# Predicting the scale of a fp16 product one batch early in a pipelined cross-attention and feed-forward kernel

## What is computed

```python
qh = Wq @ layernorm(x)                 # 512 x 1024, 8 heads of 64
kh, vh = Wk @ ctx, Wv @ ctx
q = softmax(qh, axis=head dim) * 64**-0.5
k = softmax(kh, axis=tokens)
context = einsum('hdn,hen->hde', k, vh)
out = Wo @ einsum('hde,hdn->hen', context, q) + bo
x = x + out / max(norm(out, channels), 1e-12) * g * sqrt(128)
x = x + layernorm(x) @ dequant(qweight, scales, zeros) + bias
```

## Time and profile before

| | |
|---|---|
| median of 3 runs | 782.26 us (781.7 to 784.06) |
| the profiled execution, its own time | 783.55 us |
| its span in the trace | 781.7 us |
| busy PE / DVE / POOL / ACT | 84% / 76% / 65% / 55% |
| mean granted TensorE clock | 0.972 of full speed |

### The profile page before, as it was taken

The page is one execution under the profiler, slowest core; times in us unless marked ns, Lnnn a source line. Parts: engine busy times, 40 slices in busy tenths (PEclk is TensorE's granted clock), DMA queues, the critical chain, the costliest instruction groups (busy, mean ns, idle before and its releaser), DMA issues.

```text
span 781.7 us, 10910 instructions
## 1 busy us (share of the span) xinstructions
PE 654.3 (84%) x3271; PEld 418.1 (53%) x3271; DVE 597.3 (76%) x929; ACT 431.6 (55%) x676; POOL 510.3 (65%) x362
## 2 busy tenths in 40 slices
PE   2888888898898989889898889889898988989664
PEld 2655556565555656555555555555565655556231
DVE  2897768887887879787887988788788878877622
ACT  2786457475545656564565747455574755456320
POOL 3273757668585757859485785948577685866641
PEclk9989899999999999999999999999999999999796
DMA  8035263443528254352725345262625434252602
GB/s 296 27 63 127 54 155 49 113 104 68 162 54 188 44 128 97 64 150 54 188 54 159 56 82 141 51 183 54 174 42 108 119 61 114 54 135 42 141 7 81
DMA packets 180982, 78.94 MB, mean 101 GB/s; under 512 B 170440, under 2 KB 172000, under 8 KB 180960
## 3 DMA queue, kind: packets, MB, share of 16 engines
q1 hardware_dynamic: 180960, 78.68, 42.8%
HBM read 28.32 MB, written 8.39 MB: 47 GB/s over the span
## 4 chain that ended last, share of the span: by engine, by line
DVE 32%; PE 32%; issue 18%; POOL 10%; ACT 5%; DMA 1%; DVEq 1%; ACTq 0%; POOLq 0%; SPq 0%
PE ps_m L918 13%; DVE q_sum L691 6%; DVE q_nmax L679 6%; DVE k_nmax L672 5%; POOL q_exp L392 4%; DVE x2n_lo L731 3%; POOL rn L444 3%; DVE stats L753 2%; PE ps_o L1018 2%; DVE q_exp L684 2%; DVE g_lo L745 2%; PE ps_k L860 2%; ACT q_tok_hi L532 2%; PE ps_k L862 2%; PE ps_k L861 2%
## 5 line engine op out<-in xcount | busy, mean ns | idle before, releaser
L402 POOL TENSOR_TENSOR q_tok_lo<-q_exp,q_tok_hi 128x1024 f16<-128x1024 f32 x64 | 136.7, 2135 | 84.4 <-ACT q_tok_hi L532 84.4
L392 POOL TENSOR_TENSOR q_exp<-q_exp,q_rec 128x1024 f32<-128x1024 f32 x64 | 122.7, 1917 | 68.4 <-DVE q_rec L696 68.4
L521 ACT ACTIVATE q_exp<-q_exp 128x512 f32<-128x512 f32 x128 | 80.8, 631 | 150.5 <-DVE q_exp L684 150.2
L516 ACT ACTIVATE k_exp<-ps_k,k_nmax 128x1024 f32<-128x1024 f32 x64 | 71.2, 1113 | 122.4 <-DVE k_nmax L672 120.1
L918 PE MATMUL ps_m<-k_t,c_t 128*128 128x512 f32 x256 | 116.4, 598 | 0.0
L672 DVE TENSOR_REDUCE k_nmax<-ps_k 128x1 f32<-128x1024 f32 x64 | 77.9, 1217 | 39.2 <-PE ps_k L862 39.2
L971 PE MATMUL ps_m<-w_int,x_lo 128*128 128x512 f16 x240 | 93.9, 391 | 13.3 <-DMA x_lo<-x2n_lo 13.2
L679 DVE TENSOR_REDUCE q_nmax<-ps_q 128x8 f32<-128x512 f32 x128 | 86.6, 677 | 13.2 <-PE ps_q L862 13.1
L972 PE MATMUL ps_m<-w_int,x_hi 128*128 128x512 f16 x240 | 93.7, 391 | 0.0
L684 DVE TENSOR_TENSOR q_exp<-ps_q,q_nmax 128x512 f32<-128x512 f32 x128 | 88.5, 691 | 4.4
L425 POOL TENSOR_TENSOR c_lo<-c_in,c_hi 128x1024 fp32r<-128x1024 f32 x16 | 37.9, 2369 | 65.8 <-ACT c_hi L600 65.8
(11 more groups left out here) (126 smaller groups left out, 1437.5 us busy)
## 6 DMA issues: line engine op xcount, KB each, us to landing
x_in<-in_x SPq DMA_DIRECT2D x16, 512.0 KB, 5.7
c_in<-in_ctx SPq DMA_DIRECT2D x16, 512.0 KB, 6.4
x_res<-in_x SPq DMA_DIRECT2D x16, 512.0 KB, 4.9
out_x<-y SPq DMA_DIRECT2D x15, 512.0 KB, 3.4
q_hi<-q_tok_hi SPq DMA_TRANSPOSE x64, 3.1
q_lo<-q_tok_lo SPq DMA_TRANSPOSE x64, 3.0
og<-in_L_ffn_qweight SPq DMA_DIRECT2D x1, 512.0 KB, 5.3
sq<-in_L_ffn_qweight SPq DMA_DIRECT2D x1, 512.0 KB, 6.2
```

The source lines that it names most:

```text
L392: nc.gpsimd.tensor_tensor(pair, pair, rec.unsqueeze(2).to_broadcast([P, 2 * HEADS, DH]), ALU.mult).then_inc(qs_done, 1)
L402: nc.gpsimd.tensor_tensor(q_tok_lo[p % 2][:], q_exp[:, 2 * p:2 * p + 2, :].rearrange("p t d -> p (t d)"), q_tok_hi[p % 2][:], ALU.subtract ...
```

## The change

G's scale is no longer taken from G. k's softmax weights sum to one, so no entry of M is larger, once normalised, than the largest absolute context value (`c_top`), and G sums 128 channels against `vo`: 128 x `c_top` x `v_top` (the largest absolute value in `vo`) bounds it. `v_top` is found once in turn 0 (two DVE reductions, one PE transpose). `c_top` is found for batch n in turn i: DVE reduces `c_in` to `c_abs` (1024 elements), PE spreads it (`spread_c`), DVE reduces the row. `fit_g` works out the scale of batch a in five small DVE operations, and `k_rec` carries it. In the next turn `g_hi` is written by DVE straight from PSUM (ACT's L595 goes), and `g_lo` by four DVE operations of 128 elements from PSUM. `g_t`, the reduction L741 and `spread_g` go. `c_hi` and `c_lo` have one buffer instead of two.

Each engine's order within a turn is new (K0' is the first k projection of batch n, M[a:b] are M's token tiles, c3 is the query pair 3 of batch c, a0 to a2 are pairs 0 to 2 of batch a):

| engine | before | after |
|---|---|---|
| PE | K0 Q0 TC0 G, K1 Q1 TC1 spread_g F0, K2 TK0 Q2 TK1 O0, K3 TK2 Q3 TK3 O1, TK4 Q4 TK5 F1a norm, TK6 Q5 TK7 F1b rn-spread, Q6 M[0:4], Q7 M[4:8] | Q0 G K1, TK0 Q1 TK1 O0 K2, TK2 Q2 TK3 F0a K3, TK4 Q3 TK5 F0b, TK6 Q4 TK7 O1, Q5 F1, Q6 norm TC0' spread_c M[0:4], Q7 rn-spread TC1' M[4:5] K0' M[5:8] |
| DVE | maxk0 shift0 x2n_lo sum c3 g_t g_abs, maxk1 scale shift1 g_lo, maxk2 shift2 sum a0 y0, maxk3 shift3 x2b, shift4 stats1 sum a1 n2, shift5 xn y1 og, shift6 sum a2 stats2 k_rec, shift7 | sum c3 shift0 g_hi g_lo x4 maxk1 x2n_lo, shift1 maxk2, shift2 sum a0 maxk3, shift3 y0 c_abs, shift4 sum a1 x2b, shift5 stats1 fit_g k_rec, y1 shift6 n2 c_top sum a2 xn, og shift7 stats2 maxk0' |
| POOL | low c2 scale c3, low c3 x2b, c_lo scale a0, y0 low a0, scale a1 rstd1 rn, low a1, x2 scale a2 layer norm chain, xn_lo y1 | layer norm chain scale c3 x2b low c3, (step 2) scale a0, low a0 c_lo, scale a1, y0 low a1, y1 rstd1 rn scale a2, xn_lo x2 low a2 |

On ACT, `exp_k(j+1)` stands in step j, x2n and x2n_hi at the head of the turn, both `squares` in step 4, and the moves of the transposed context in steps 6 and 7. SP stores y in the turn in which it is made, before the last query pair's transposes. The weights' split into high and low parts moves behind c_hi (ACT, DVE), and the set-up of the rows into turn 0.

The diff, cut to its core (16 columns of indentation taken off):

```diff
-G_FLOOR = 1e-25
-G_RANGE = 2.0 ** 8
+UNIT_FLOOR = 1e-30
+G_RANGE = 2.0 ** 15
...
-c_hi = [sb(f"c_hi{s}", [P, N], F32R) for s in range(2)]
-c_lo = [sb(f"c_lo{s}", [P, N], F32R) for s in range(2)]
+c_hi = sb("c_hi", [P, N], F32R)
+c_lo = sb("c_lo", [P, N], F32R)
...
+    if f > 0:
+        sp.wait_ge(y_ready, 2 * f)
+    sp.dma_start_transpose(x2_hi[:], x2n_hi[:]).then_inc(x2hi_turned, 16)
 if do_c:
-    turn_q(c, 3, ("hi", "lo"))
+    turn_q(c, 3, "hi")
+if do_f:
+    sp.wait_ge(x2lo_done, f + 1)
+    sp.dma_start_transpose(x2_lo[:], x2n_lo[:]).then_inc(x2lo_turned, 16)
+if do_c:
+    turn_q(c, 3, "lo")
 if do_a:
-    turn_q(a, 0, ("hi", "lo"))
-    turn_q(a, 1, ("hi", "lo"))
-    turn_q(a, 2, ("hi",))
-if f == NB - 1:
+    for p in range(2):
+        turn_q(a, p, "hi")
+        turn_q(a, p, "lo")
+if do_f and f < NB - 1:
+    sp.wait_ge(y_done, 2 * (f + 1))
+    sp.dma_start(out[f], y[:]).then_inc(y_stored, 16)
+elif do_f:
     for h in range(2):
         sp.wait_ge(y_done, 2 * f + h + 1)
         sp.dma_start(halves(out[f])[h], halves(y)[h]).then_inc(y_stored, 16)
+if do_a:
+    turn_q(a, 2, "hi")
+    turn_q(a, 2, "lo")
 for i in range(FIRST, LAST):
...
+    if j == 6 and do_c:
         pool.wait_ge(n2_moved, c + 1)
         nc.gpsimd.tensor_tensor(rn[:], n2[:], neg_half[:], ALU.pow).then_inc(rn_done, 1)
...
+    if j == 6 and do_a:
+        scale_q(a, 2)
+    if j == 7 and do_n:
+        pool.wait_ge(xnhi_done, n + 1)
+        if begun(8 * a):
+            pool.wait_ge(q_ready, 8 * a)
+        nc.gpsimd.tensor_tensor(xn_lo[1 - s][:], xn[:], xn_hi[1 - s][:].bitcast(F32),
+                                ALU.subtract).then_inc(xnlo_done, 1)
+    if j == 7 and do_c:
         for h in range(HALVES):
...
             nc.gpsimd.tensor_tensor(halves(x2)[h], halves(og)[h], halves(x_res)[h],
                                     ALU.add).then_inc(x2_done, 1)
...
+if isinstance(i, int) and i == FIRST:
     set_up()
 for j in range(STEPS):
+    if j == 4 and isinstance(i, int) and i == FIRST:
+        set_up_rest()
     if j == 0 and do_c:
         act.wait_ge(m_ready, c + 1)
         if begun(c):
             act.wait_ge(g_ready, c)
         nc.scalar.activation(m_t[:], ps_m[:], ACT.Copy).then_inc(m_moved, 1)
-    if j in (3, 4) and do_c:
-        squares(j - 3)
-    if j < HC and do_a:
-        exp_k(j)
-    if 2 <= j < 6 and do_a:
-        move_tk(2 * (j - 2))
+    if j == 0 and do_a:
+        exp_k(0)
+    if j == 0 and do_f:
+        act.wait_ge(rstd2_steps, 4 * (f + 1))
+        if begun(f):
+            act.wait_ge(nrs_done, f)
+        nc.scalar.activation(x2n, x2[:].rearrange("p (r t) -> p t r", t=2), ACT.Identity,
+                             bias=nmr2[:], scale=rstd2[:], accum_out=rs2[:]).then_inc(x2n_done, 1)
+    if 1 <= j < 5 and do_a:
+        move_tk(2 * (j - 1))
+    if j in (1, 2) and do_a:
+        move_tk(2 * (j - 1) + 1)
     if do_a:
         exp_q(j)
-    if j < 2 and do_a:
-        move_tc(j)
-    if 2 <= j < 6 and do_a:
-        move_tk(2 * (j - 2) + 1)
-    if j == 1 and do_c:
+    if j == 0 and do_f:
+        act.wait_ge(x2n_done, f + 1)
+        if begun(f):
+            act.wait_ge(x2hi_turned, 16 * f)
+            act.wait_ge(x2lo_done, f)
+        nc.scalar.activation(x2n_hi[:], og[:], ACT.Copy).then_inc(x2hi_done, 1)
+    if j == 0 and do_c:
         high_q(c, 3)
-        act.wait_ge(gfit_steps, 5 * c + 3)
-        if begun(2 * c):
-            act.wait_ge(out_ready, 2 * c)
-        nc.scalar.activation(g_hi[:], g_t[:], ACT.Identity, scale=g_fit[:]).then_inc(ghi_done, 1)
-    if j == 2 and do_n:
+    if j < 3 and do_a:
+        exp_k(j + 1)
+    if j in (3, 4) and do_a:
+        move_tk(2 * (j - 1) + 1)
+    if j == 3 and do_a:
+        high_q(a, 0)
+    if j == 3 and do_n:
         act.wait_ge(c_loaded[1 - s], loads(n, 1 - s))
-        if begun(8 * (n - 1)):
-            act.wait_ge(k_ready, 8 * (n - 1))
-        nc.scalar.activation(c_hi[1 - s][:], c_in[1 - s][:], ACT.Copy).then_inc(chi_done, 1)
-    if j in (3, 5) and do_a:
-        high_q(a, (j - 3) // 2)
+        if begun(8 * n):
+            act.wait_ge(k_ready, 8 * n)
+        nc.scalar.activation(c_hi[:], c_in[1 - s][:], ACT.Copy).then_inc(chi_done, 1)
+    if j == 4 and do_c:
+        squares(0)
+        squares(1)
+    if j == 4 and do_a:
+        high_q(a, 1)
+    if j in (6, 7) and do_n:
+        move_tc(j - 6)
     if j == 6 and do_n:
         act.wait_ge(xn_done, n + 1)
         if begun(8 * a):
             act.wait_ge(q_ready, 8 * a)
         nc.scalar.activation(xn_hi[1 - s][:], xn[:], ACT.Copy).then_inc(xnhi_done, 1)
-    if j == 7 and do_c:
-        act.wait_ge(rstd2_steps, 4 * (c + 1))
-        if begun(c):
-            act.wait_ge(nrs_done, c)
-        nc.scalar.activation(x2n, x2[:].rearrange("p (r t) -> p t r", t=2), ACT.Identity,
-                             bias=nmr2[:], scale=rstd2[:], accum_out=rs2[:]).then_inc(x2n_done, 1)
-    if j == 7 and do_a:
+    if j == 6 and do_a:
...
+def fit_g():
+    if isinstance(i, int) and i == 0:
+        dve.wait_ge(vtop_done, 1)
+    dve.wait_ge(ctop_done, a + 1)
+    nc.vector.tensor_scalar(g_unit[:], c_top[:], v_top[:], P / G_RANGE, ALU.mult,
+                            ALU.mult).then_inc(fit_steps, 1)
+    dve.wait_ge(fit_steps, 5 * a + 1)
+    nc.vector.tensor_scalar(g_unit[:], g_unit[:], UNIT_FLOOR, None, ALU.max).then_inc(fit_steps, 1)
+    dve.wait_ge(fit_steps, 5 * a + 2)
+    nc.vector.reciprocal(g_fit[:], g_unit[:]).then_inc(fit_steps, 1)
+    if do_c:
+        dve.wait_ge(og_done, 2 * (c + 1))
+    nc.vector.tensor_scalar(g_undo[:], g_unit[:], 1.0 / Q_RANGE, None, ALU.mult).then_inc(fit_steps, 1)
+    dve.wait_ge(fit_steps, 5 * a + 4)
+    nc.vector.tensor_tensor(gs_undo[:], g_undo[:], gs_col[:], ALU.mult).then_inc(fit_steps, 1)
...
+    if j == 0 and do_c:
+        sum_q(c, 3)
+    if j == 6 and do_f:
+        scale_y(1)
+    if j == 7 and do_c:
+        for h in range(HALVES):
+            dve.wait_ge(rb_ready, 2 * c + h + 1)
+            dve.wait_ge(og_done, 2 * c + h + 1)
+            nc.vector.tensor_tensor(halves(og)[h], halves(og)[h], ps_o[h][:],
+                                    ALU.mult).then_inc(att_done, 1)
     if do_a:
         shift_q(j)
+    if j == 0 and do_c:
+        dve.wait_ge(krec_done, 2 * (c + 1))
+        dve.wait_ge(g_ready, c + 1)
+        if begun(2 * c):
+            dve.wait_ge(out_ready, 2 * c)
+        nc.vector.tensor_tensor(g_hi[:], ps_o[0][:].rearrange("p (c o) -> p c o", c=HC),
+                                k_rec[:].unsqueeze(2).to_broadcast([P, HC, P]),
+                                ALU.mult).then_inc(ghi_done, 1)
+        dve.wait_ge(ghi_done, c + 1)
+        for fc in range(HC):
+            nc.vector.scalar_tensor_tensor(out=g_lo[:, fc, :], in0=ps_o[0][:, fc * P:(fc + 1) * P],
+                                           scalar=k_rec[:, fc:fc + 1], in1=g_hi[:, fc, :],
+                                           op0=ALU.mult, op1=ALU.subtract).then_inc(glo_done, 1)
+    if j < 3 and do_a:
+        if j == 2:
+            sum_q(a, 0)
+        max_k(a, j + 1)
     if j == 0 and do_f:
         dve.wait_ge(x2hi_done, f + 1)
         if begun(f):
             dve.wait_ge(x2lo_turned, 16 * f)
         nc.vector.tensor_tensor(x2n_lo[:], og[:], x2n_hi[:], ALU.subtract).then_inc(x2lo_done, 1)
...
+    if j == 3 and do_n:
+        dve.wait_ge(c_loaded[1 - s], loads(n, 1 - s))
+        if begun(n):
+            dve.wait_ge(cabs_ready, n)
+        nc.vector.tensor_reduce(c_abs[:], c_in[1 - s][:], op=ALU.max, axis=AX_X,
+                                apply_absolute_value=True).then_inc(cabs_done, 1)
+    if j == 4 and do_a:
...
+    if j == 5 and do_a:
+        dve.wait_ge(kexp_done, 4 * (a + 1))
+        nc.vector.reciprocal(k_rec[:], k_sum[:, s, :]).then_inc(krec_done, 1)
+        fit_g()
+        dve.wait_ge(krec_done, 2 * a + 1)
+        nc.vector.tensor_scalar(k_rec[:], k_rec[:], g_fit[:], q_scale, ALU.mult,
+                                ALU.mult).then_inc(krec_done, 1)
+    if j == 5 and do_n:
         nc.vector.bn_aggr(mv1[:], stats1[:].rearrange("p a b -> p (a b)")).then_inc(stats1_done, 1)
...
+    if j == 6 and do_n:
+        dve.wait_ge(cabs_ready, n + 1)
+        nc.vector.tensor_reduce(c_top[:], ps_o[1][:, 0:P], op=ALU.max, axis=AX_X).then_inc(ctop_done, 1)
+    if j == 6 and do_a:
+        sum_q(a, 2)
+    if j == 6 and do_n:
...
+    if j == 7 and do_c:
         if begun(4 * c):
             dve.wait_ge(rstd2_steps, 4 * c)
         for h in range(HALVES):
             dve.wait_ge(x2_done, 2 * c + h + 1)
             nc.vector.bn_stats(stats2[:, h, :], halves(x2)[h]).then_inc(stats2_part, 1)
...
+    if j == 7 and do_n:
+        max_k(n, 0)
+    if j == 7 and do_c:
         nc.vector.bn_aggr(mv2[:], stats2[:].rearrange("p a b -> p (a b)")).then_inc(stats2_done, 1)
...
 for j in range(STEPS):
-    if j < HC and do_a:
-        project_k(j)
-    if 2 <= j < 6 and do_a:
-        transpose_k(2 * (j - 2))
+    if 1 <= j < 5 and do_a:
```

(60 more changed lines are left out.)

290 lines of the change are left out of this document (123 added, 167 removed).

## The result

Against the kernel before, timed on the same chip, the changed kernel takes 792.83 us (median of 4 runs, 791.91 to 795.76) where the kernel before takes 782.57: a ratio of 1.013, interval 1.0112 to 1.0148. That is a small loss, clear of the noise. The forecast was 759, and its range ended at 776.

The account below looks back on a forecast made before the run. Neither PE (84% busy) nor DVE (76%) was full; they hand each other work and both pause. Savings of 15.6 + 3 + 0.5 + 0.5 + 4 = 23.6 us from 783.55 gave 760.0, as a median about 759 us, range 742 to 776.

Parts of the forecast that it names:

- turns 2 to 14: Thirteen turns, Q0 to Q0, each 43.8 us instead of 45.01, 1.2 less: 15.6 us saved.
- turn 0: First turn, 36.7 us before: new v_abs, v_top and c_abs (2.5) set against K waits of 2 to 3: -0.5.
- turn 1: Second turn, 44.5 us before: no stage f, so x2b, x2n_lo and y not in its way: some 41.5, -3.
- turn 15 to M's end: Last turn: has no K0' to hide, -0.5.
- M's end to the spread of rn, drain: After the last M: m_t earlier, g_abs and g_hi chain gone; about 26 us becomes 22, -4.
- DVE's sum: DVE's busy time per turn, 36.64 us before, adding removed, new and held operations: 37.0 us.
- DVE's waits: DVE's waits per turn for K2, K3, y0, og and x2: together 6.1 us, plus 0.7 of small gaps.
- the ring: Loop through x2, its statistics, maxk0 and shift0; its largest wait, the statistics waiting for POOL's x2, was put at 2.9 us.
- The step that failed: PE does as much as before, 39.4 us busy per turn, so 4 us of slack makes its own waits free.
- K0' amid M: Next batch's first k projection inside M: M hides K0, removing DVE's 2.60 us wait for it.
- The slower rival: x2 on POOL comes late through xn_lo or rn, lengthening the ring; turns from 45.6 us, e.g. 46.2 and 790 us; chance 0.09.
- C: Theory that x2 stands behind xn_lo on POOL and the ring over x2 sets the turn; The slower rival, chance 0.09.

Follow-up runs that it names:

- e1: Changed kernel plus nine constant-operand matmuls, result unread, on PE in the pause between F1 and Q6: 779.31 us, ratio 0.9949.
- e10: e9 with ten constant-operand matmuls, result unread, ahead of PE's wait for the two ACT copies: 792.77 us, ratio 1.0109.
- e7: Kernel before, in its order, with G's new scale; c_abs ends step 4, its spread inside F1b, c_top before xn: 761.43 us, ratio 0.9725.
- e9: e7 with PE made to wait, ahead of the spread of rn, for two unread ACT copies started when F1 ends: 797.04 us, ratio 1.0163.
- e5: Changed kernel with PE's sixteen one-column sums of squares moved from behind Q6 to ahead of F1's last two token tiles: 780.04 us, ratio 0.9952.
- e11: e7 with the next batch's first k projection placed amid M and DVE's maximum of it at the turn's end: 759.59 us, ratio 0.9696.
- e8: e5 with POOL's x2 put ahead of xn_lo: 796.79 us, ratio 1.0136.
- e4: Kernel before, in its own order, with only G's new scale; c_abs ahead of xn, its spread ahead of rn's: 774.82 us, ratio 0.9879.

## Why the prediction was wrong

By its own steps, against the spans, which differ by 790.3 - 781.7 = +8.6 us where -23.6 was forecast. The 32.2 us between them lie here:

| step | forecast | measured | missed by |
|---|---|---|---|
| turns 2 to 14 | -15.6 | +8.9 | 24.5 |
| turn 0 | -0.5 | +3.7 | 4.2 |
| turn 1 | -3.0 | -2.5 | 0.5 |
| turn 15 to M's end | -0.5 | -1.3 | -0.8 |
| M's end to the spread of rn, drain | -4.0 | +1.2 | 5.2 |
| before Q0 of batch 0, and behind rn | 0 | -1.3 | -1.3 |

**DVE's sum was right.** Forecast 37.0 us of work per turn, measured 37.19. The four `g_lo` take 1.13 in all (forecast 0.8, and 2.12 before). L722 is held by c_lo for 1.4 us (forecast 1.3), although it had never been held in the trace of before. Going by k_rec was the right choice, and what the prediction drew from the Trainium skill, SBUF — State Buffer, Who interferes with whom, that the loser "fully blocks", agrees with this trace: `q_rec` ends 0.03 us behind POOL's c_lo.

**DVE's waits were too low**, 8.5 us per turn against 6.8. On average K2 takes 1.1 and K3 1.2 (forecast 0.85 and 0.6), y0 0.75 (0.85), `og` 3.3 (0.9) and x2 0.3 (2.9). `og` and x2 together are 3.7 against 3.8, so the long wait of the ring was right in size, but it stands for PE's spread of rn and not for POOL's x2. Waits for c_top (0.6) and n2 (0.1) were not in the sum, and the small gaps are 1.1 (0.7).

**The step that failed** is the sentence "At 39.4 busy it has 4 us of slack per turn, so what it waits for costs nothing by itself". Both halves of it are wrong.

- PE's busy time is not fixed. It rose to 42.44 us for the same matmuls, since part of them ran at 0.50 of the clock. That takes 3.0 of the 4 us of slack. Its cost: with the pause filled (e1) the turns are 44.70 instead of 45.69, 1.0 us per turn and 13 of the 24.5 us. The changed kernel's own turns agree. The three in which only M is slow have a mean of 44.65, with `og` waiting 2.5 to 2.6 us; the three in which Q6 is slow from its start have 46.77, with `og` waiting 4.0 to 4.2.
- A wait of PE costs its full length when it stands ahead of something DVE waits for. In e10 a delay of 1.4 us ahead of the spread made `og` 1.4 us late, at the full clock.

The other 0.9 us per turn (11.6 us of the 24.5) is there at the full clock too. In e1 the sum of a turn is 37.1 of DVE's work, 2.5 for K2 and K3 (forecast 1.45), 0.75 for y0, 3.3 for `og` and x2 (forecast 3.8) and 1.1 of small gaps (0.7). So the waits for K2 and K3 are the largest term that was too small. What sets them was not tested; they are no shorter in e7 (2.4 and 0.7), whose turns are 43.39 in the old order. By DVE's rows e7 gains its time elsewhere: it is busy 36.1 us per turn, 1.0 less than in e1, with 0.8 instead of 2.1 for the four `q_rec`.

Why the clock costs so little in e9: there the slow stretch begins with the spread of rn, or behind it, so at most the spread's 0.9 us (1.97 against 1.09) lie ahead of `og`. In the changed kernel Q6, the sums of the squares, TC0', the spread of c_abs, M[0:4] and Q7 all stand between the pause and the spread of rn; the two of them with rows above are 3.6 us longer. This was argued from the timelines. e5, which takes the sums out of that stretch, fits it: in its turns at the full clock `og` waits 1.0 us. Whether the pause or the one-column sums behind it bring the clock down in the changed kernel is open. A kernel with the one and without the other was not run; e1 has the sums and no pause, and there M's first half was slow in seven turns of thirteen.

**K0' amid M** was counted as a wait of 2.6 us gone. e11 shows 0.02 us per turn for it on its own. DVE's next need, Q0, stands behind M just as K0 did. The prediction listed x2 as what is late next and did not look at Q0.

**Turn 0.** The forecast had v_abs, v_top and c_abs, 2.5 us, hidden in DVE's waits. DVE was busy 37.88 us in it, 31.57 before. To these three come c_top (0.3) and the rows' set-up, which moved in from ahead of Q0 (1.3 us of it; the section on the change says so, and the sum passed over it), and holds by POOL:

```profile
42.98 2.13 DVE L722 TENSOR_SCALAR q_rec<-q_rec 128x16 f32<-128x16 f32 x1
...
49.02 1.75 DVE L740 TENSOR_TENSOR gs_undo<-g_undo,gs_col 128x1 f32<-128x1 f32 x1
```

PE waited 4.54 us for a subtraction behind the first.

**The drain.** G follows M after 0.69 us (4.57 before) and O0 stands 2.09 us behind it, much as forecast. But rn did not come earlier:

```profile
736.67 1.09 PE L999 MATMUL ps_o<-vo,m_t 128*64 128x128 f32 x16 [0.69 <-ACT m_t L590]
739.86 0.59 PE L915 MATMUL ps_o<-q_hi,g_lo 128*128 128x512 f16 x1 [2.09 <-issue]
...
747.09 0.59 PE L1035 MATMUL ps_m<-w_int,x_lo 128*128 128x512 f16 x1 [3.03 <-issue]
...
763.43 1.97 PE L1089 MATMUL ps_o<-ident,rn 128*128 128x128 f32 x8 [2.06 <-POOL rn L463]
```

In the new order F0 stands between O0 and O1, and F0 waits 3.03 us for x2's transposed parts (x2n, now at the head of ACT's turn, had itself waited 1.98 us for POOL's nmr) and its first 14 matmuls are recorded at 0.59 to 0.63 us each, where one at the full clock has 0.38. Then the sums of the squares stand behind all of F1. The forecast counted what had gone from the chain and not what had moved into it.

**The slower rival** had the right sign at 0.09 and the wrong mechanism (C, which e8 refutes). The prediction's list of what would show it wrong did name the place, PE idle ahead of Q6 or M, but set the limit at 3 us and read it as a sign about DVE; the trace has 2.3.

## What to carry over

Before an engine's idle time is called slack, go through what stands behind each of its waits and who needs that: in this pipeline PE's wait ahead of a result that DVE was about to ask for cost its whole length (e10). Then ask what it would cost if the clock fell to a half behind that wait: nothing where something else is late anyway (M in e1), 3 us per turn where nothing is (e8). And see, as e5 did, whether the one-column matmuls there can stand elsewhere. When single turns are compared, check that they hold the same operations. And when a change bundles a new algorithm with a new order, try the algorithm in the old order first: here that was 2.7% faster (e7), the bundle 1.3% slower.

## What was not expected of the hardware

- The granted clock fell to 0.50 behind a pause of 2.3 us in the changed kernel (at once in some turns, only for M in others), behind one of 2.88 us in nine turns of thirteen in e9, and behind one of 2.20 us in one turn of e8 but not behind one of 2.30 in another. It did not fall behind pauses of 1.73 and 1.80 us in the kernel before, whose turns are at 1.00. In e4 it fell behind waits of 0.47 and 1.29 us in eight turns of thirteen, and in e1 with 0.26 us of idle time in 14. So the length of one pause does not decide by itself.
- The holds go both ways. With DVE's x2n_lo begun first (1.22 us), POOL's low_q behind it took 3.20 us, against 2.13 or 2.14 for the three others of that turn:

```profile
338.11 1.22 DVE L787 TENSOR_TENSOR x2n_lo<-og,x2n_hi 128x1024 f16<-128x1024 f32 x1
```

```profile
338.14 3.20 POOL L406 TENSOR_TENSOR q_tok_lo<-q_exp,q_tok_hi 128x1024 f16<-128x1024 f32 x1
```

- An operation on a single column (L740, 128x1) is held like a large one: 1.75 us in turn 0, where it takes 0.16 in the turn at 331.62.
